# VectorE instead of GpSimd makes the low halves of the three context chunks

## The reference

```python
ln_out = _ln(hidden_states, ln_w, ln_b)
q = _ln(_fp8_linear_pertensor(ln_out, wq, ...).reshape(b, s, g, hpg, d), qln_w, qln_b)
k, v, qx = ...                                      # in the same way
kvx = jnp.einsum('bsi,oi->bso', cond, w_kv_x)       # the context, in full precision
kx, vx = jnp.split(kvx, 2, axis=-1)
kx = _ln(kx.reshape(b, sc, g, d), kxln_w, kxln_b)
core = _gqa(q, k, v)                                # softmax attention
xout = _gqa(qx, kx, vx)
catq = _div_clamp_fp8(jnp.concatenate([core, xout], axis=-1), proj_smooth)
return jnp.einsum('bsi,oi->bso', catq, wproj) * (proj_in_scale * proj_w_scale)
```

## Time and profile before

| | |
|---|---|
| median of 3 runs | 1267.72 us (1266.91 to 1267.89) |
| profiled execution | 1270.7 us, its span 1268.9 us |
| TensorE matmuls busy | 1125.3 us, 89% of the span |
| VectorE busy | 862.6 us, 68% |
| ScalarE busy | 698.3 us, 55% |
| GpSimd busy | 481.8 us, 38% |
| mean granted TensorE clock | 0.955 |

### The profile page before, as it was taken

One profiled execution on the slowest core, in us unless ns is written; L12 is line 12 of the kernel. 1 busy time (PEld: TensorE's weight loads), 2 busy tenths in 40 slices (PEclk: granted clock), 3 DMA queues, 4 the chain that ended last, 5 costly groups with the idle time before them and its releaser, 6 DMA issues. The chain is left out here.

```text
span 1268.9 us, 22397 instructions
## 1 busy us (share of the span) xinstructions
PE 1125.3 (89%) x5792; PEld 909.2 (72%) x5792; DVE 862.6 (68%) x1740; ACT 698.3 (55%) x1746; POOL 481.8 (38%) x608
## 2 busy tenths in 40 slices
PE   1089999979999998999998999998799939999996
PEld 1068777767787776778776888886688727777775
DVE  7978778886778787887888778777444765655100
ACT  7965677854666784566776556555112413334442
POOL 3074344343344434443444444442000222655432
PEclk9599999999999999999999999999899859999998
DMA  5041111114111112411111311110546066766220
GB/s 192 20 173 46 32 39 49 41 33 167 32 55 40 33 32 61 162 41 31 48 43 30 132 37 51 40 36 11 182 142 240 22 227 191 217 183 188 46 42 1
DMA packets 51715, 107.36 MB, mean 85 GB/s; under 512 B 5984, under 2 KB 26464, under 8 KB 49568
## 3 DMA queue, kind: packets, MB, share of 16 engines
q1 hardware_dynamic: 46912, 97.00, 23.5%
q0 software_dynamic: 4704, 9.18, 3.3%
HBM read 91.48 MB, written 16.52 MB: 85 GB/s over the span
## 5 line engine op out<-in xcount | busy, mean ns | idle before, releaser
L721 PE MATMUL p_proj<-w_hi,xqs 128*112 128x256 f32 (+1 forms) x512 | 173.4, 358 | 57.0 <-DVE w_lo L495 47.7
L569 POOL TENSOR_TENSOR c_lo<-c_raw,c_hi 128x500 fp32r<-128x500 f32 x96 | 122.4, 1275 | 175.4 <-ACT c_hi L609 175.4
L730 PE MATMUL p_proj<-w_hi,c_hi 128*125 128x512 f32 x384 | 166.2, 433 | 9.3 <-DVE w_lo L495 8.2
L559 POOL TENSOR_TENSOR va<-ss,epst 112x4 f32<-112x4 f32 (+2 forms) x192 | 74.1, 386 | 261.7 <-DVE ss L862 261.7
L721 PE MATMUL p_proj<-w_lo,xqs 128*112 128x256 f32 (+1 forms) x512 | 163.7, 339 | 0.0
L563 POOL TENSOR_TENSOR rs<-va,mhalf 112x4 f32<-112x4 f32 (+2 forms) x192 | 155.5, 810 | 18.0 <-POOL va L559 5.8
L730 PE MATMUL p_proj<-w_hi,c_lo 128*125 128x512 f32 x384 | 152.6, 397 | 0.0
L730 PE MATMUL p_proj<-w_lo,c_hi 128*125 128x512 f32 x384 | 152.4, 397 | 0.0
L721 PEld LDWEIGHTS p_proj<-w_hi,xqs 128*112 128x112 f32 x512 | 90.1, 176 | 73.7 <-issue 55.6
L862 DVE TENSOR_REDUCE ss<-sq 112x4 f32<-112x512 f32 (+2 forms) x192 | 96.2, 504 | 52.6 <-ACT sq L630 51.7
L658 ACT ACTIVATE pcross<-p_cross,nmax 112x375 f32<-112x375 f32 x128 | 73.2, 574 | 82.7 <-DVE nmax L891 82.0
(11 more groups left out here) (230 smaller groups left out, 2720.6 us busy)
## 6 DMA issues: line engine op xcount, KB each, us to landing
c_raw<-in_ctxT SPq DMA_DIRECT2D x96, 250.0 KB, 2.6
shared<-in_w_in SPq DMA_DIRECT2D x16, 1024.0 KB, 9.1
shared<-in_wproj SPq DMA_DIRECT2D x32, 256.0 KB, 2.9
raw_g<-in_Wg SPq DMA_DIRECT2D x8, 1024.0 KB, 6.6
raw_u<-in_Wu SPq DMA_DIRECT2D x8, 1024.0 KB, 7.6
raw_d<-in_Wd SPq DMA_DIRECT2D x8, 1024.0 KB, 5.6
cat_scratch<-cat SPq DMA_DIRECT2D x32, 224.0 KB, 2.0
shared<-cat_scratch SPq DMA_DIRECT2D x2, 1792.0 KB, 8.0
```

The source lines that it names most:

```text
L559: pool.tensor_tensor(va[0:rows, lo:hi], ss[0:rows, lo:hi], epst[0:rows, lo:hi], ALU.add).then_inc(va_done, 1)
L569: pool.tensor_tensor(flat(c_lo[:, k, :, :]), flat(c_raw[:, k, :, :]), flat(c_hi[:, k, :, :]).bitcast(F32), ALU.subtract).then_inc(cl_done, 1)
L721: m = pe.matmul(bank[0:T, o:o + w], xqs[:, n, k, :], (w_hi, w_lo)[i % 2][:, k, lo:lo + w], start=(i == 0), stop=(i == 2 * KB - 1))
L730: m = pe.matmul(bank[0:CT, :], a[:, ch, k, :], w[:, k, CKX:CV], start=(i == 0), stop=(i == 3 * KB - 1))
```

## The change

The three subtractions of a step go from GpSimd's order to VectorE's, with the same waits and the same semaphore. On VectorE they stand in three places: the first between the maxima of the first two heads' cross scores, the second behind the scale of nqx, the third behind the scale of nk. In step 0 they stand ahead of the sums.

```diff
     @block.gpsimd
     def _(pool):
-        pool.sem_inc(cl_done, 3)
...
-        def c_low(s, k):
-            pool.wait_ge(ch_done, 3 * (s + 1) + k + 1)
-            pool.wait_ge(pj_rdy, 6 * s + 4 + k)
-            pool.tensor_tensor(flat(c_lo[:, k, :, :]), flat(c_raw[:, k, :, :]),
-                               flat(c_hi[:, k, :, :]).bitcast(F32), ALU.subtract).then_inc(cl_done, 1)
...
-            for j in range(3):
-                c_low(s, j)
-                rstd(s, j)
-            for j in range(3, 6):
+            for j in range(6):
                 rstd(s, j)
...
     @block.vector
     def _(v):
+        v.sem_inc(cl_done, 3)
...
+        def c_low(s, k):
+            v.wait_ge(ch_done, 3 * (s + 1) + k + 1)
+            v.wait_ge(pj_rdy, 6 * s + 4 + k)
+            v.tensor_tensor(flat(c_lo[:, k, :, :]), flat(c_raw[:, k, :, :]),
+                            flat(c_hi[:, k, :, :]).bitcast(F32), ALU.subtract).then_inc(cl_done, 1)
...
             if A: scale(s, 0)
             if Q: max_cross(t, 0)
+            if A: c_low(s, 0)
             if Q: max_cross(t, 1)
...
             if A: scale(s, 1)
+            if A: c_low(s, 1)
             if Q: take_cross(t, 1)
             if Q: max_cross(t, 3)
             if A: scale(s, 2)
+            if A: c_low(s, 2)
...
                 smooth_of(g)
+                for j in range(3):
+                    c_low(s, j)
                 for j in range(6):
                     sums(s, j)
```

## The result

The changed kernel takes 1336.24 us in the median (1335.57 to 1337.27, 4 runs), the kernel before 1267.81 us on the same chip (1266.91 to 1268.79, 4 runs). The ratio is 1.0536, with a 95% interval of 1.0515 to 1.0557: 5.4% slower, 68 us. The prediction was 1342 us, range 1320 to 1364. The profiled execution took 1337.3 us with a span of 1335.0 us, 66.1 more than before; the mean granted clock was 0.952 against 0.955.

The account below looks back on a forecast made before the run. In the attention part TensorE was taken to bound the time, each wait before its matmuls paid in full unless already waiting. 70.0 - 7.6 + 12 = +74 us gave 1342 us, range 1320 to 1364.

Parts of the forecast that it names:

- The relief: Subtractions leaving GpSimd: 0 gained by itself for TensorE; VectorE's nq and nqx scales fall to 0.68 us each.
- The first wait: Before the fourth projection TensorE waits for the first low half on VectorE: 1.23 us per ordinary step.
- The second wait: Before the fifth projection TensorE waits for the second low half: 1.77 us, 1.57 after 0.20 for the dry matmul queue.
- The third one: Third subtraction, behind the scale of nk: ends before the sixth projection, cost 0; up to 0.60 us a step if uncovered.
- Returns in centring steps: In 12 weight-centring steps VectorE's means come 0.63 us earlier against TensorE: 7.6 us back, bounds 0 and 17.
- Weight changes: Six steps at a change of weights cost 2.0 us more each, 12 us in all.
- Step 0 and the rest: Step 0's three subtractions: cost 0, bounds -1 and +2; GpSimd's DMAs and SyncE's loads: cost 0.
- The forecast's own bounds: Its terms were said to give 1332 to 1351 us: restarts -5 and +5, weight steps -3 and +4.
- (a): Not slower: VectorE's relief, 22.8 us on nq alone, outweighs the added subtractions; 1262 to 1268 us, chance 0.03.
- (c): More comes back: centring steps catch up entirely, another 10 us, and weight changes cost 1; about 1326 us, chance 0.17.
- (d): Third subtraction's cover fails, or VectorE's longer loop body costs time at branches: 15 us more, 1357 us, chance 0.11.
- (b): GpSimd's power, starting just before nq, holds VectorE's port so nq ends 0.9 us later: 28 us more, 1370 us, chance 0.11.

Follow-up runs that it names:

- early placements: Changed kernel with the first subtraction between the first two sums, the second ahead of the self-transpose copy, or both: ratios 1.0175, 1.0283, 0.9970 to the kernel before.
- relief alone: Kernel before, with GpSimd after step 0 subtracting one column of 500 and leaving the other 499 out; ratio 0.9844 to the kernel before.
- both early: Changed kernel with the first subtraction between the first two sums and the second ahead of the self-transpose copy; ratio 0.9970 to the kernel before.
- first early: Changed kernel with only the first subtraction moved on VectorE, to between the first and second sums; ratio 1.0175 to the kernel before.
- Third twice: Changed kernel with one more subtraction of the same shape, into a scratch tile, ahead of the third; ratio 1.0602 to the kernel before.
- Port held: Changed kernel with GpSimd also making a 128x500 subtraction of other data at the three old places; ratio 1.0679 to the kernel before.
- GpSimd swap: Kernel before, with inverse root 1 put ahead of the second subtraction in GpSimd's order; 1259.5 us, ratio 0.9936 to the kernel before.
- second early: Changed kernel with only the second subtraction moved on VectorE, to ahead of the self-transpose copy; ratio 1.0283 to the kernel before.

## Why the prediction was right, point by point

**What bounds, and that each wait is paid in full: right.** Two waits a step, by VectorE's c_lo, never a third, 85% busy for TensorE (about 84 foreseen). The early placements take each wait away by itself, so the cause is shown and not only argued.

**The relief, 0 by itself: right where TensorE sets the step, incomplete elsewhere.** nq and nqx take 0.68 as foreseen. The run with the relief alone shows 20 us, of which 12.4 at the weight changes. My sum had some of this as returns (7.6) and within the 12 for weight changes, but the sentence that the removals gain 0 holds only where TensorE and not VectorE sets the step, in steps 26, 28 and 30 to 0.02 us.

**The first wait, 1.23: measured 1.11.** c_low took 0.67; the restart was 0.14 (625.88 to 626.02), not the middle of 0.15 and 0.35 that I took. The lower of the two rows was right.

**The second wait, 1.57: measured 1.65 - 0.22 = 1.43.** The restart again (0.15), and the queue of earlier matmuls, run dry in the wait, gave back what I had allowed for it (0.20): 4.94 instead of 5.16. Together 2.54 instead of 2.80 a step. This is the term that was off by most: 25 x 2.80 = 70 should have been 25 x 2.54 = 63.5, and not all of the 25 steps pay even that: the 12 ordinary ones took 2.31 more on the mean.

**The third one, 0: right in the changed kernel, for the reason given,** since the two pauses let VectorE catch up. With the pauses gone, "both early" shows 0.21 a step.

**Returns in centring steps, 0.63 each: measured 2.54 - 1.92 = 0.62 each.** The size is right to the hundredth, but by some luck in the working: the means start 4.05 us after the fifth projection, 0.81 earlier than 4.86, and 0.22 of that is the dry queue that every step gets. In the terms found above: the way to the means grew from 19.16 to 21.11 us, and the step by as much. Three ordinary steps behind a centring one (7, 15, 23) returned some 0.6 as well, and steps 1, 3, 11 and 19 some 0.1 to 0.3, which I had not counted.

**Weight changes, 12: measured 12.7, partly by luck.** It came unevenly, +4.0 us in step 8 and -0.4 in step 9, and an estimated 3.4 us of it is clock, which my working didn't have (see the end); the waits themselves are nearer 9.

**Step 0 and the rest, 0: +1.7 in step 0.** It isn't the subtractions on VectorE: with the relief alone, where step 0 has its full subtractions on GpSimd as before, step 1 also starts at 85.8 us instead of 84.1. In all runs but the kernel before it starts between 84.8 and 87.0. Most of it is clock. Step 0 before, in the changed kernel and with first early (stretch, us, busy times of TensorE, its weight loads, VectorE, ScalarE and GpSimd, granted clock, DMA share, GB/s):

```profile
65.00:84.10 19.10, 16.17 (x69) 12.68 (x69) 15.14 (x16) 9.41 (x19) 17.46 (x14) 0.89 0.25 73
```

```profile
65.20:85.78 20.58, 18.15 (x69) 14.54 (x69) 15.15 (x19) 9.40 (x19) 14.51 (x12) 0.79 0.48 176
```

```profile
65.75:84.83 19.08, 16.01 (x69) 12.53 (x69) 15.11 (x19) 9.41 (x19) 14.44 (x12) 0.90 0.45 159
```

0.2 of the 1.7 us lies ahead of the step's first matmul. The step itself is 1.48 us longer where the clock is lower, and as long as before with first early, whose subtractions stand where the changed kernel has them. Third twice (19.12 us, 0.89) agrees. Port held is 1.4 us longer at 0.91, but there VectorE is busy for 17.27 us of the step. Why one run has the lower clock and another doesn't is open.

**The forecast's own bounds.** They give 1334 and not 1332 at the lower end: 1342 less 5 less 3. The bounds that I had named for the returns (0 and 17) and for step 0 (-1 and +2) are not in them. The stated range, 1320 to 1364, doesn't hang on this.

**The rivals.** (a) fell: without a wait TensorE would have been at 615.58 + 9.33 = 624.91 and at 628.90 + 2.09 = 630.99, and the low halves were ready at 625.88 and 632.49. (c) and (d) fell by the rows above. (b), the port held by the power, fell in the changed kernel, on the row that was to decide it:

```profile
624.04 1.01 POOL L562 TENSOR_TENSOR rs<-va,mhalf 112x4 f32<-112x4 f32 x1
```

The power starts 0.11 us before nq (624.15), runs beside all of it, and nq keeps its 0.68, as it does in all 32 steps (0.68 or 0.69). In 16 of them it is the other way round: where the power starts from 0.01 us before nq to 0.29 behind it, the power takes 1.26 to 1.56 us instead of 1.01 and ends 0.86 to 0.88 behind the scale. Step 21:

```profile
651.50 1.56 POOL L562 TENSOR_TENSOR rs<-va,mhalf 112x4 f32<-112x4 f32 x1 [0.16 <-POOL va L558]
```

```profile
651.51 0.68 DVE L868 TENSOR_TENSOR nq<-nq,rs 112x512 f32<-112x512 f32 x1
```

The Trainium skill (SBUF — State Buffer, Who interferes with whom) has such a pair lock for the whole instruction, the first to issue winning. For the 128x500 subtraction the rows agree that the scale is held to its end, and in these 16 steps the power is delayed by the scale. For a power that starts 0.09 to 0.11 us earlier they don't show a lock for the whole instruction: it still runs for the whole of nq and delays nothing. The measurement decides for this kernel.

## What to carry to other kernels

In this kernel an operation off the critical path cost nothing by its own length on the slow engine (what it cost, about 1.6%, came through the scales that it held), and its full length plus everything that stands before it in the queue on the engine that feeds the bottleneck: 1275 ns on GpSimd delayed no matmul directly, 671 ns on VectorE cost 5.4%, and the same 671 ns in other places of its order cost nothing. When the work of two engines holds each other up, look first at which neighbour it meets: exchanging two neighbours on GpSimd gave 0.6%, and exchanging one more pair turned that into 2.0% lost. And find, for each kind of step, the one event whose time sets its length (here TensorE in ordinary steps, VectorE's means in centring steps, 5.4 us ahead of the end): what moves that event is the price of an edit.

## What the runs showed of the hardware that I had not expected

**A long wait of TensorE can be followed by half clock.** At the weight change of step 8 TensorE waits 4.38 us for c_lo, and its matmuls then stand 0.43 us apart instead of 0.23. The changed kernel's TensorE and the stretch, in the columns used above:

```profile
289.64 0.76 PE L720 MATMUL p_proj<-w_hi,c_hi 128*125 128x512 f32 x1 [4.38 <-DVE c_lo L845]
290.20 0.63 PE L720 MATMUL p_proj<-w_lo,c_hi 128*125 128x512 f32 x1
290.63 0.63 PE L720 MATMUL p_proj<-w_hi,c_lo 128*125 128x512 f32 x1
```

```profile
289.60:295.00 5.40, 5.36 (x13) 4.09 (x14) 2.04 (x7) 2.69 (x9) 0.00 (x0) 0.50 0.19 47
```

0.50 is 1.2 of 2.4 GHz, for all 12 matmuls of the projection, at a price of 12 x 0.20 = 2.4 us. In the kernel before, the same place had a wait of 2.74 us and full clock; in the kernel with the GpSimd swap a wait of 2.75 us at the same place and half clock for most of the stretch. Before, then with the swap:

```profile
272.00:276.40 4.40, 3.08 (x13) 2.19 (x13) 3.69 (x7) 2.58 (x13) 3.71 (x4) 1.00 0.22 58
```

```profile
271.80:276.30 4.50, 4.45 (x13) 3.48 (x14) 3.79 (x8) 3.76 (x16) 3.59 (x4) 0.62 0.00 0
```

The kernel before has three stretches of its own at 0.50 in these steps (9, 16 and 24). Those in steps 16 and 24 lie at this same place, behind waits of 2.74 and 2.73 us:

```profile
304.80:308.20 3.40, 3.40 (x11) 2.48 (x11) 2.50 (x6) 1.63 (x5) 1.91 (x3) 0.50 0.99 401
482.30:485.70 3.40, 3.40 (x10) 2.43 (x9) 3.33 (x6) 2.01 (x11) 2.71 (x3) 0.50 0.29 74
690.50:693.90 3.40, 3.40 (x11) 2.25 (x10) 3.33 (x8) 2.01 (x9) 2.33 (x3) 0.50 0.29 75
```

So the same wait was followed by full clock in step 8 and by half clock in steps 16 and 24 of one and the same run. All nine waits of 4.4 us at this place (changed kernel, second early, third twice) were followed by matmuls 0.37 to 0.44 us apart on the mean, the three of 1.7 us with the relief alone by 0.24. The length of the wait alone doesn't decide it, and nothing here settles what does.

Half of 3.4 us is 1.7, and by about so much, for each such stretch that comes or goes, the sums over weight-change steps and step 0 are uncertain. In its six weight-change steps the changed kernel has 17.0 us at 0.50, the kernel before 10.2 and the relief alone none. By this estimate 3.4 of the 12.7 us that the change costs there are clock, and 5 of the 12.4 that the relief alone gains.

**A scale that has started can be held by a subtraction that starts after it in the trace** (2.04 us instead of 0.68 above, and 2.04 to 2.13 in 31 of 32 steps of that run), and every scale that was held, in three kernels, ended 0.54 or 0.55 us behind the subtraction's end. So the start that the trace gives for the subtraction can't be the moment that decides. The last attention step with the GpSimd swap shows it most plainly, GpSimd and then VectorE:

```profile
850.70 1.26 POOL L569 TENSOR_TENSOR c_lo<-c_raw,c_hi 128x500 fp32r<-128x500 f32 x1
```

```profile
849.82 2.69 DVE L873 TENSOR_TENSOR nq<-nq,rs 112x512 f32<-112x512 f32 x1
```

The subtraction starts 0.88 us behind the scale, which takes 0.68 alone and would have been done by then; it ended at 852.51, 0.55 behind the subtraction. In both runs GpSimd's power was running when the scale started and the subtraction stood right behind the power; powers alone held no nq or nqx in the changed kernel.
